# Edge bias of the tail: from a VectorE add to a ScalarE write into the PSUM bank that TensorE adds to

## What is computed

```
h = relu(layernorm(x))
in_deg, out_deg = counts of dst and of src, clamped to 511
sum3d = segment_sum(edge_attr @ W_sum + b_sum, src)
out = x + h + z_in[in_deg] + z_out[out_deg]
        + sigmoid(cent @ W_cent + b_cent) + sigmoid(vor @ W_vor + b_vor) + sum3d
```

## Time and profile before

| | us |
|---|---|
| runs | 3068.52, 3068.58, 3073.89 (median 3068.58) |
| the profiled execution | 3061.41 |
| its span | 3059.6 |
| first z_out gather, last z_out gather | 2832.38, 3049.52 |
| last DVE add | 3056.33 |

### The profile page before, as it was taken

The page is one execution under the profiler, slowest core; times in us unless marked ns, Lnnn a source line. Parts: engine busy times, 40 slices in busy tenths (PEclk is TensorE's granted clock), DMA queues, the critical chain, the costliest instruction groups (busy, mean ns, idle before and its releaser), DMA issues.

```text
span 3059.6 us, 41787 instructions
## 1 busy us (share of the span) xinstructions
PE 1690.0 (55%) x9095; PEld 1297.1 (42%) x9095; DVE 1777.5 (58%) x6055; ACT 771.3 (25%) x3973; POOL 1857.0 (61%) x1869
## 2 busy tenths in 40 slices
PE   4645545555555333555554555555555566667776
PEld 1234333444344222444444444444444455555655
DVE  6555456666666532555655665544444455558878
ACT  3322222333233331332332332222222222200111
POOL 5666666656555665555555565555656565567787
PEclk7656677666656555777767777777777677879888
DMA  4255333334444443555555555556556566679896
GB/s 126 86 147 159 103 105 109 107 110 132 117 131 123 138 127 111 150 159 147 165 145 156 161 169 148 167 168 169 165 165 173 148 189 186 187 180 235 209 238 174
DMA packets 499624, 465.45 MB, mean 152 GB/s; under 512 B 74023, under 2 KB 459181, under 8 KB 499372
## 3 DMA queue, kind: packets, MB, share of 16 engines
q1 hardware_dynamic: 417326, 313.53, 39.5%
q0 software_dynamic: 78752, 136.44, 14.1%
q10 hardware_dynamic: 3294, 12.80, 1.3%
HBM read 332.60 MB, written 129.73 MB: 151 GB/s over the span
## 4 chain that ended last, share of the span: by engine, by line
another core or an unknown queue 33%; DVE 22%; PE 16%; issue 13%; ACT 5%; DMA 4%; POOL 4%; DVEq 2%; SPq 0%; POOLq 0%; ACTq 0%
PE bank L994 8%; ACT junk L868 5%; DVE hot_n L670 4%; POOL sorted L513 3%; DVE hot_dh L605 3%; DVE acc L697 3%; DMA edge_ring<-in_L_gnn_z_out_dram,out_i 3%; DVE hot_dl L605 3%; PE bank L942 2%; PE bank L977 1%; DVE gate_normed L736 1%; PE bank L971 1%; DVE hot_t L605 1%; PE bank L978 1%
## 5 line engine op out<-in xcount | busy, mean ns | idle before, releaser
L513 POOL DMA_INDIRECT sorted<-edge_ring,pos_i x1660 | 1600.5, 964 | 1112.1 <-DVE pos_i L803 632.9
L994 PE MATMUL bank<-piece_ring,hot_n 128*125 128x129 f32 x5320 | 959.0, 336 | 328.7 <-DVE hot_n L670 248.9
L994 PEld LDWEIGHTS bank<-piece_ring,hot_n 128*125 128x125 f32 x5320 | 882.9, 240 | 460.6 <-DVE hot_n L670 300.3
L868 ACT ACTIVATE junk<-bank,mark_col 128x100 bf16<-128x100 f32 x1664 | 548.5, 341 | 1828.8 <-remote 1385.4
L697 DVE TENSOR_TENSOR acc<-bank,acc 125x129 f32 x1330 | 376.3, 283 | 701.0 <-remote 534.8
L670 DVE SCALAR_TENSOR_TENSOR hot_n<-bank,wkey,piece_ring 128x250 f32<-128x250 f32 x1330 | 621.5, 468 | 10.1 <-DMA piece_ring<-sorted 8.9
L977 PE MATMUL bank<-hot_w,after_b 128*128 128x400 bf16 x416 | 187.2, 450 | 629.2 <-ACT junk L868 472.8
L1019 PE MATMUL bank<-hot_dl,hot_dh 128*125 128x100 bf16 x1661 | 212.6, 280 | 273.7 <-DVE hot_dh L605 235.6
L868 ACT ACTIVATION_READ_ACCUMULATOR junk<-bank,mark_col 128x1 f32 x1664 | 337.0, 203 | 5.1 <-issue 5.1
L977 PEld LDWEIGHTS bank<-hot_w,after_b 128*128 128x128 bf16 x416 | 50.1, 120 | 673.0 <-ACT junk L868 502.0
L605 DVE TENSOR_TENSOR hot_dl<-dst_parts,bank 128x400 bf16<-128x400 bf16 x416 | 146.0, 351 | 317.8 <-remote 281.9
(11 more groups left out here) (107 smaller groups left out, 1205.2 us busy)
## 6 DMA issues: line engine op xcount, KB each, us to landing
piece_ring<-sorted SPq DMA_DIRECT2D x1330, 130.0 KB
edge_ring<-in_edge_attr_dram SPq DMA_DIRECT2D x332, 320.0 KB
sorted<-edge_ring,pos_i POOLq DMA_INDIRECT x1660
base<-in_x_dram SPq DMA_DIRECT2D x20, 560.0 KB
out_dram<-base ACTq DMA_DIRECT2D x19, 560.0 KB
out_dram<-base SPq DMA_DIRECT2D x9, 560.0 KB
base<-out_dram SPq DMA_DIRECT2D x9, 560.0 KB
edge_ring<-in_L_gnn_z_out_dram,out_i POOLq DMA_INDIRECT x100
```

The source lines that it names most:

```text
L513: g.indirect_dma_start(rows, bass.IndirectOffsetOnAxis(index, 0), edge_ring[:, slot, at, :], None).then_inc(s_scatter[slot], 16)
L868: last = a.activation(junk[:, t, :], part[:, t // 2, :, t % 2], ACT.Relu, bias=mark_col[:, :], accum_out=pos_f[:, q % 4, t:t + 1])
L994: last = t_.matmul(to, hot_n[:, n % HOT_SLOTS, k, :], piece_ring[:, n % PIECE_SLOTS, k, 0:SUM], start=(k == 0), stop=(k == ROW_GROUPS[s] - 1))
```

## The change

DVE's bias add is gone. In its place ACT writes b_sum times the count (an ACTIVATE Identity with a per-partition scale) to ps_y[w % 2], and PE's product adds to what stands there (start=False). For this PE writes both banks once, by two 128x256 products with the identity, ahead of the last segment's pieces. The wait of product w for the add of product w - 2 moves from PE to ACT's bias write, and PE waits for that write.

```diff
@@ tail_adds
-                       + [(ahead + BIAS_LAG + w, "bias", w) for w in range(NW)]
@@ vector, add_to_row
-                if kind == "bias":
-                    dve.wait_ge(s_summed, piece0[NS - 1] + ahead + w + 1)
-                    last = v.scalar_tensor_tensor(out=row, in0=rows_b[0:NODE_P, 4, :], scalar=acc[0:NODE_P, w, F:SUM], in1=row,
-                                                  op0=ALU.mult, op1=ALU.add)
-                elif kind == "product":
+                if kind == "product":
@@ scalar
+            def bias(w):
+
+                act.wait_ge(s_summed, piece0[NS - 1] + ahead + w + 1)
+                if w == 0:
+                    act.wait_ge(s_y_bank, 1)
+                elif w >= 2:
+                    act.wait_ge(s_added, added["product", w - 2])
+                a.activation(ps_y[w % 2][0:NODE_P, 0:D], rows_b[0:NODE_P, 4, :], ACT.Identity,
+                             scale=acc[0:NODE_P, w, F:SUM]).then_inc(s_bias, 1)
+
             for w in range(NW):
+                bias(w)
                 copy_sum(w)
@@ tensor, product
                 pe.wait_ge(s_sumT_sb, n + 1)
-                if n >= 2:
-                    pe.wait_ge(s_added, added["product", n - 2])
-                t_.matmul(ps_y[n % 2][0:NODE_P, 0:D], sumT[:, n % 2, :], w_sb[:, :], start=True, stop=True).then_inc(s_y, 1)
+                pe.wait_ge(s_bias, n + 1)
+                t_.matmul(ps_y[n % 2][0:NODE_P, 0:D], sumT[:, n % 2, :], w_sb[:, :], start=False, stop=True,
+                          skip_group_check=True).then_inc(s_y, 1)
@@ tensor, ahead of the tail's loop
+            pe.wait_ge(s_in_deg, 1)
+            pe.wait_ge(s_node, NW)
+            for b in range(2):
+                last = t_.matmul(ps_y[b][0:NODE_P, 0:D], ident[:, 0:NODE_P], rows_b[:, 4, :], start=True, stop=True)
+            last.then_inc(s_y_bank, 1)
```

More of the change, by code:

```diff
@@ L54 @@
 PRODUCT_LAG = 5
-BIAS_LAG = 5
 ADD_LAG = 7
@@ L358, in gnn_kernel @@
         s_y = sem("s_y")
+        s_bias = sem("s_bias")
+        s_y_bank = sem("s_y_bank")
         s_added = sem("s_added")
@@ L774, in add_to_row @@
                     dve.wait_ge(s_guest[(w - ROW_SLOTS) // X_WINDOWS], 64)
-                before = [added[kind_, w] for kind_ in ("z_in", "bias", "product", "z_out") if added[kind_, w] < added[kind, w]]
+                before = [added[kind_, w] for kind_ in ("z_in", "product", "z_out") if added[kind_, w] < added[kind, w]]
                 if before:
                     dve.wait_ge(s_added, max(before))
-                if kind == "bias":
-                    dve.wait_ge(s_summed, piece0[NS - 1] + ahead + w + 1)
-                    last = v.scalar_tensor_tensor(out=row, in0=rows_b[0:NODE_P, 4, :], scalar=acc[0:NODE_P, w, F:SUM], in1=row,
-                                                  op0=ALU.mult, op1=ALU.add)
-                elif kind == "product":
+                if kind == "product":
                     dve.wait_ge(s_y, w + 1)
```

## The result

| | before | changed |
|---|---|---|
| median of runs, us | 3068.58 (7 runs, 3066.46 to 3077.33) | 3049.14 (7 runs, 3040.68 to 3057.11) |
| profiled execution, us | 3061.41 | 3052.17 |
| its span, us | 3059.6 | 3050.4 |
| first z_out gather to last DVE add, us | 2832.38 to 3056.33 = 223.95 | 2834.91 to 3046.27 = 211.36 |

The ratio is 0.9935 [0.9917, 0.9952], so 19.4 us less, with an interval of 14.7 to 25.5. The forecast was 3060.8, its range ended at 3052. The direction is right, the size is not. The two profiled executions differ by only 9.2 us: the tail is 12.6 shorter, but it began 2.5 us later and 0.9 more stands behind the start of its last add. Of the executions of the experiments, one of e11 (3586 us) and one of the kernel before beside it (3967 us) lie far above all others and do not enter the ratios.

The account below looks back on a forecast made before the run. DVE and POOL were taken as near each other, POOL's 1.50 us per gather leaving 16.4 us at most. Terms -3.0 - 2.0 - 3.5 + 0.7 = -7.8 us gave 3060.8 us; 8-in-10 range 3052 to 3072.

Parts of the forecast that it names:

- The step of DVE: Removing one scalar_tensor_tensor in each of 100 steps saves 0.40 us per step; in C 1.71 falls to 1.31 us.
- B: Tail's 109.99 us middle stretch, 69 gathers, POOL bound; fewer long gathers give 2.0 us, a third of 6.5.
- C: Tail's 46.02 us last stretch, after the guests; POOL becomes the bound, gain 3.5 of 5.5 us.
- A: Tail's 22.37 us stretch from 2871.14, DVE busy throughout; gain 3.0 us, ends 0 and 4.4.
- The link through ACT: Product waits for add, bias write, then sumT copy, about 0.75 us; costed at nothing, hidden by two-step lags.
- The second limit: z_out added five steps after out_i: landings keep five steps at 8.4 us or more in A, 7.5 in C.
- PE's two bank writes: Two 128x256 products ahead of the tail, on PE's path; cost 0.7 us, ends 0 and 2.4.
- Landings: Rival, chance 0.24: later landings leave A and B no gain and C 2.0 us; 3067.3 us.
- The free port case: Rival, chance 0.09: removing the two-SBUF-input instruction frees the shared port, all floors reached, -15.7 us; 3052.9 us.
- The slower case: Rival, chance 0.14: new link binds at low clock, 0.6 us on each of 17 products, +7.9 us; 3076.5 us.

Follow-up runs that it names:

- e11: Kernel before with out_i one step earlier and the z_out add two steps later; 2465.96 us against 2477.49, ratio 0.9954.
- e9: Changed kernel with z gathers of 64 rows instead of 125; 2415.13 us against 2477.49 for the kernel before, ratio 0.9748.
- e10: Kernel before with z gathers of 64 rows instead of 125; 2430.52 us against 2477.49, ratio 0.9809.
- the repeats: The changed kernel run again twice (e5, e13), with e6 as the kernel before; ratios 0.9946 and 0.9954.
- e14: Kernel before with the bias add dropped and nothing in its place; 2461.27 us against 2473.33, ratio 0.9952.
- e13: Changed kernel a third time, against the kernel before; 2462.26 us against 2473.33, ratio 0.9954.
- e7: Changed kernel with ACT's copy of sumT ahead of the bias write; 2467.86 us, 7.3 us slower than e5.
- e2: Changed kernel with an extra unused DVE operation like the old bias add, both inputs in SBUF; 2476.63 us against 2472.78 before, ratio 1.0012.
- e8: Changed kernel with out_i one step earlier and the z_out add two steps later; 2454.45 us against 2473.46 before, ratio 0.9922.
- e15: Changed kernel with out_i one step earlier and the z_out add two later, again; 2455.66 us against 2473.33 before, ratio 0.9932.
- e1: Kernel before with DVE's bias add reading b_sum from PSUM instead of SBUF; 2473.49 us against 2472.78, ratio 1.0003.
- e3: Changed kernel with an extra unused DVE operation, one input in PSUM and one in SBUF; 2474.75 us against 2472.78 before, ratio 1.0007.
- e5: Changed kernel once more, against the kernel before in the same job; 2460.58 us against 2473.46, ratio 0.9946.
- e12: Changed kernel with an extra 125x64 DVE operation per window, one input in PSUM; 2468.43 us against 2477.49 before, ratio 0.9966.
- e6: Kernel before against itself, for its profile; 2473.75 us against 2473.46, ratio 0.9995.

## Why the forecast was right in kind and wrong in size

**What held.** The step of DVE fell by 0.39 us (0.40 forecast); 40 us of its time gave 12.6 of the tail, because POOL's 1.50 us for each gather lets no more than 16.4 through (e9 shows that POOL is the limit after in B and C, e10 that it was before in B). A gave 3.0 in the first pair and 3.2 in the repeats (3.0 forecast). The link through ACT was costed at nothing, and no cost of it can be told from the scatter (1.0 us, e14 against e13), though the bias write takes 0.478 instead of 0.39 and the product comes 0.85 us after the add instead of 0.75. It is hidden only in the order given, as e7 turns it into 7.3 us, and beside the shorter step of DVE, as e2 shows. The second limit that the forecast named for A and C, the landing within a fixed number of steps, is real: e8 and e15 moved it and gained 6 us, in the profiled e8 3.2 of them on the 36 gathers ahead of B (57.80 to 54.62).

**The step that failed** is the term for B: "I take a third of the 6.5 us, 2.0". The mechanism named there (long gathers, fewer when DVE has pauses) is the one found, and it was mis-sized, the third having no reason given: B gave 4.7 us in the first pair and 3.3 and 3.9 in the repeats, some 50 to 70% of what was to be had. C, 3.5 forecast, gave 4.1, and 5.2 and 6.5 in the repeats, the last at its floor. The 0.7 us for PE's two bank writes can't be seen (the time from the first tail gather to the first z_out gather went from 105.0 to 105.6 and 105.2 us in the repeats, and from 113.2 to 111.5 in the first pair). The terms as measured in the first pair make 0.5 + 3.0 + 4.7 + 4.1 + 0.3 = 12.6 where 7.8 stood. The forecast missed the measured 19.4 us by 11.6: 4.8 of that are the tail's, and 6.8 lie outside of all its terms and are not explained. A gain of 12.6 would have left the time within the range.

**What was missed in the traces of before.** The forecast read the long gathers by their longest and their mean, and looked for the cause in "DVE without a pause". Reading each one with the DVE row at its start would have given the law above, and from it why the excess is so large: in C a DVE step is 1.71 us. A gather held to the end of a z add starts its successor 1.37 us behind that end (-0.13 + 1.20 + 0.30); the next z add ends 1.71 behind it, so the next gather is held by 1.71 - 1.37 - 0.13 = 0.21 again, 1.41 us, which is what the earlier trace rows has. A step of 1.65 makes it 1.34 or 1.35, and the five gathers above alternate so. By this arithmetic POOL is caught by DVE's step as long as that is longer than 1.50; with steps of 1.32 and 1.25 it can't be, and gathers start in z adds only by chance. The five rows show the catch itself. That it explains the counts elsewhere agrees with e1 to e3 (55 to 61 gathers in z adds, 0.23 to 0.25 us each) and with e5 and e13 (46 and 34, 0.12 and 0.11 each), but was not tested by itself; e12, with steps of 1.48 us on average and an excess of 6.8, shows that the excess does not drop at once where the step comes under 1.50.

**The rivals.** Landings did come later, up to 11.09 us, and the tail gained all the same; but with more lead there are 6 us to be had on the changed kernel (e8, e15) and 11.5 on the one before (e11). The free port case got its time (3049.1 against 3052.9) but not by its reason: the gathers are short now with the z adds' ports in use as ever, and e1 freed the bias's port for nothing. The slower case came in a small way: DVE waited 8.8 us for products, 0.5 before, and the tail ends at the lower clock. The last 8 us of the changed kernel and of its repeat e13 ran at a granted 0.50, but e5's did not:

```profile
2449.81:2457.81 8.00, 1.81 (x8) 0.98 (x7) 2.79 (x7) 1.03 (x3) 2.08 (x2) 0.84 0.77 228
```

(e5; windows view, the clock is the third number from the end.) e5's last gather needed 6.82 us to its add, e13's and the changed kernel's 6.62 and 6.56, so at the very end it decided nothing.

**What stays open.** Tails differ by 12.6, 9.6 and 11.9 us, and the repeats' times by 12.9 and 11.1. The first measurement gave 19.4 [14.7, 25.5]. The 7 us or so beyond the tail are not in the profiled pair (9.2 us). The runs behind it scatter by 11 us before and 16 after, and the profiled run before lay 7.2 us under its median and below all seven runs, where the forecast took its difference to the median as it was. Whether the change helps something ahead of the tail on a chip that runs the program in 3069 us, or whether this is scatter, no run here tells.

## What to carry to other kernels

The time taken off one engine was worth here only what the next engine's rate let through, stretch by stretch, so floors come first; but what the second engine loses to the first (here gathers held by adds) is part of what can be had, and it is found by putting every instruction that is longer than the least beside what the other engine does at its start. Two pieces of work on one engine that a third waits for cost nothing here while the one that is ready first stood first (the bias write before the copy). And where a result is awaited at a fixed lag, try the lag: two numbers gave 6 us here on the changed kernel and 11.5 on the one before, as much as the change itself.

## What the runs showed of the hardware

- A gather issued by POOL is long only if DVE is in an add with both tensors in SBUF at its start (before: 58 of 68 such gathers, none of the other 65), and it is held until 0.13 us before that add's end. Where another such add followed directly, it was held to the end of that one in 12 of 15 cases before, and to the first one's in the other 3. Of all gathers of 125 rows in the 15 tails that were profiled with them, one began 0.02 us ahead of a z add and was held too (e5, 1.51 us); no other that started outside such an add was.
- POOL's cost of a gather depends on its rows, but not in proportion: 0.91 us for 64 and 1.20 for 125, with 0.30 to the next.
- An ACTIVATE of 125x256 from SBUF into PSUM takes 0.478 us, 128x125 from PSUM 0.276 and 125x512 into PSUM 0.601: the straight line between the last two gave 0.39. The bias write has a per-partition scale, which the other two have not; whether the 0.09 us are its price was not tried.
- The same program took 3069 us in one measurement and 2473 in others, with nearly the same tail. POOL's scatters (L513) waited 632.9 us for pos_i (L803) in the first and 36.0 in e6, a difference that is about that of the two times. What made pos_i late is not shown. ACT's waits are named differently, the first row below being that of before, the other two that of e6: where one has 1385 us for something that the profile does not name, the other has 1166 us for the landings of edge_attr, in L875:

```profile
L868 ACT ACTIVATE junk<-bank,mark_col 128x100 bf16<-128x100 f32 x1664 | 548.5, 341 | 1828.8 <-remote 1385.4
```

```profile
L868 ACT ACTIVATE junk<-bank,mark_col 128x100 bf16<-128x100 f32 x1664 | 546.4, 339 | 179.1 <-PE bank L971 176.8
```

```profile
ACT edge_ring L875 <- DMA edge_ring<-in_edge_attr_dram: 1165.6, 300, 16.4
```
